# The second layer's experts computed for each token's two choices, in 15 sorted tiles, in place of all eight experts for all tokens

## The chip, the cores and the metric

The kernel runs on one core of one Trainium2 chip. A core has TensorE (matmuls, recorded as PE, its weight loads as PEld), VectorE (DVE), ScalarE (ACT), GpSimd (POOL) and SyncE (SP, which only issues DMAs). Each engine takes its own instructions in order; semaphores order the engines among each other. The metric is the device time of one execution in microseconds; less is better.

## The reference

Eight batches of 512 tokens with 128 features pass two layers. Each layer is a mixer and a mixture of experts, each behind a layer norm with a learned shift and scale, and each result is gated and added to x. Layer 0's mixer is causal attention, layer 1's a state-space scan (256 channels, 16 states). Layer 0's experts are small (64 hidden units). What the change touches is layer 1's expert block, with E = 8, F = 512, D = 128, TOP_K = 2:

```python
logits = xf @ gate_w
top_w, top_idx = jax.lax.top_k(logits, TOP_K)
top_w = jax.nn.softmax(top_w.astype(jnp.float32), axis=-1).astype(x.dtype)
combine = jnp.zeros((t, e), x.dtype).at[jnp.arange(t)[:, None], top_idx].add(top_w)
h = jax.nn.gelu(jnp.einsum('td,edf->tef', xf, w1) + b1, approximate=False)
y = jnp.einsum('tef,efd->ted', h, w2) + b2
out = jnp.einsum('ted,te->td', y, combine)
```

The reference computes every expert for every token; `combine` is zero but for two experts of each token.

## The kernel before

All tensors are fp32 but for some small bf16 operands. A batch is one iteration; the instruction streams of the five engines are written out by hand, and the order in each stream is the order of work. Batch b goes through three stages:

- attention of layer 0: 32 units (`UNITS`, numbered n), each a score matmul with a mask matmul (L701, L703), a row maximum on VectorE (L1335), an exponential on ScalarE (L1006) and transposes (L711). Between the units stand pieces of batch b - 1: the end of its mixer, its last layer norm (`norm_step`, j = 3), its choice of experts (`expert_head`, at the units in `PE_HEAD`, `ACT_HEAD`, `DVE_HEAD`), and `finish` of batch b - 2 (at unit `FINISH`), which gates the sum of the experts (L1181) and adds x (L1184).
- the middle stage: output of attention, layer norm 1, router and experts of layer 0, layer norm 2 (j = 2; rows normalised at L1214, transposed at L586), input projection, convolution, softplus. In between, projections of batch b + 1, and expert work of batch b - 1 by `early`.
- the scan of layer 1, 16 steps over two halves: decays on ScalarE (L1078), injected inputs and sums on GpSimd (L447, L466), `tensor_tensor_scan` and a product on VectorE (L1482, L1162), sums on TensorE (L663, L872). GpSimd injects three steps ahead. Between the steps TensorE does expert pieces of batch b - 1 (`SCAN_HIDDEN`, `SCAN_OUTPUT`), ScalarE gelus (`SCAN_GELU`, between two table loads) and VectorE additions (`SCAN_ADD`).

Layer 1's experts before: for each of 8 experts, 4 matmuls of 128 hidden units by 512 tokens (`hid1`, L602), a gelu with bias each (L933), and for each of 4 token tiles 4 accumulating matmuls of 128 columns (`out1`, L618). VectorE adds each expert's tile to `expert_sum`, scaled by the token's gate (`add_expert`, L1174). `w1` and `w2` (2 MB each) are loaded at the start and stay. The last batch has no later batch to stand beside: its experts follow its scan.

SP's queue carries, for each batch, the copies of the keys of batch b + 1 (`place_keys`, L379), then the rows that are broadcast for the scan (`spread_rows`, L407, 512 KB each, eight a batch). GpSimd's queue carries loads of x, stores of results, the gating of weights, and then its part of the scan (`sum_states`).

## Time and profile before

| | us |
|---|---|
| median of 3 runs | 1379.67 (1378.98 to 1379.79) |
| the profiled execution | 1379.79 |
| its span, first to last instruction | 1379.8 |
| a batch, from one scan's start to the next | 157.8 to 159.4 |
| mean granted TensorE clock | 0.950 |

A window's row gives start:end, length, each engine's busy us and records (x), granted clock, DMA share and GB/s; a sum or mean row runs over several windows. "Busy" is the time in which at least one instruction of the engine or group ran; the mean of one can be longer, because instructions overlap in the pipeline.

### The profile page before, as it was taken

The page shows a single profiled execution, that of the slowest core. Times are in us where ns is not written, and L with a number is a line of the kernel's source. Part 1 is how long each engine was busy: PE and PEld are TensorE (multiplying, and loading weights), DVE is VectorE, ACT ScalarE, POOL GpSimd, SP SyncE. Part 2 cuts the span into 40 slices and gives each one's busy share as a digit, 9 for nine tenths or more (in the row PEclk, how much of TensorE's full clock was granted, in tenths as well). Part 3 has the DMA queues.
Part 4 walks back from the last instruction along what each step waited for, and adds up shares of the span by engine and source line. Part 5 has one row for each costly group of instructions (what it writes and reads, how often), then busy time and mean ns, then how long its engine had stood idle before and what let it go on. Part 6 is the DMA issues. An engine that isn't in the chain of part 4 may idle for free. (4 is left out here: it accounts for less than half of the span.)

```text
span 1379.8 us, 19465 instructions
## 1 busy us (share of the span) xinstructions
PE 1207.2 (87%) x6560; PEld 760.5 (55%) x6560; DVE 1037.0 (75%) x2381; ACT 852.2 (62%) x1600; POOL 489.3 (35%) x309
## 2 busy tenths in 40 slices
PE   5974689989998889989999889989899899889698
PEld 3651145655665556555656456655656556555456
DVE  3666977599866997589866997579975998569822
ACT  2634446488646966489565866479664876469332
POOL 0103930078002950069100960049300870029300
PEclk8995579999999999999999999999999999999899
DMA  7101100030001200020001200021000300011000
GB/s 245 70 16 64 60 8 1 16 108 16 16 17 55 69 12 6 16 92 31 17 9 43 88 1 17 16 78 47 16 1 16 109 16 9 1 64 60 8 1 8
DMA packets 18514, 53.22 MB, mean 39 GB/s; under 512 B 4976, under 2 KB 5864, under 8 KB 18032
## 3 DMA queue, kind: packets, MB, share of 16 engines
q1 hardware_dynamic: 16112, 43.40, 9.8%
q0 software_dynamic: 1296, 4.20, 1.0%
q10 hardware_dynamic: 1008, 4.38, 0.8%
q8 instruction: 53, 0.87, 0.3%
q14 instruction: 45, 0.37, 0.1%
HBM read 45.40 MB, written 2.38 MB: 35 GB/s over the span
## 5 line engine op out<-in xcount | busy, mean ns | idle before, releaser
L1482 DVE TENSOR_TENSOR_SCAN probs_T<-bank,probs_T 128x512 f32<-128x512 f32 x256 | 303.9, 1212 | 16.1 <-ACT bank L1078 12.1
L618 PEld LDWEIGHTS bank<-w_w,hidden 128*128 128x128 f32 x2048 | 248.8, 192 | 72.9 <-issue 66.8
L602 PE MATMUL bank<-hT,w_w 128*128 128x512 f32 x512 | 262.9, 629 | 27.1 <-ACT hidden L933 26.2
L447 POOL TENSOR_TENSOR probs_T<-step_space,probs_T 128x1024 f32<-128x1024 f32 x120 | 282.2, 2358 | 5.9 <-DVE probs_T L1482 5.7
L618 PE MATMUL bank<-w_w,hidden 128*128 128x128 f32 x2048 | 251.6, 276 | 2.1 <-DVE expert_sum L1174 1.6
L933 ACT ACTIVATE hidden<-bank,w_b 128x512 f32<-128x512 f32 x256 | 169.6, 686 | 117.5 <-PE bank L602 116.9
L1006 ACT ACTIVATE probs<-bank,row_neg 128x128 f32<-128x128 f32 (+3 forms) x256 | 134.8, 528 | 151.7 <-DVE row_neg L1335 134.8
L1078 ACT ACTIVATE bank<-step_space,a_neg 128x512 f32<-128x512 f32 x256 | 167.8, 683 | 55.0 <-DVE probs_T L1482 36.7
L701 PE MATMUL bank<-k_pad,q_lat 128*128 128x512 f32 (+3 forms) x512 | 185.3, 448 | 5.8 <-DMA k_pad<-xc 5.8
L1335 DVE TENSOR_REDUCE row_neg<-bank 128x1 f32<-128x128 f32 (+3 forms) x256 | 123.5, 487 | 85.1 <-PE bank L703 82.7
L602 PEld LDWEIGHTS bank<-hT,w_w 128*128 128x128 f32 x512 | 89.0, 194 | 153.0 <-ACT hidden L933 97.0
L466 POOL TENSOR_TENSOR step_space<-step_space,probs 128x512 f32<-128x512 f32 x112 | 142.1, 1269 | 66.2 <-DVE probs L1162 66.1
L663 PE MATMUL bank<-probs,w_ident 128*128 128x512 f32 x256 | 146.0, 654 | 9.1 <-DVE probs L1162 9.1
L1162 DVE TENSOR_TENSOR probs<-probs_T,bank 128x1024 f32<-128x1024 f32 x128 | 153.2, 1197 | 0.4 <-PE bank L663 0.3
L711 PE MATMUL bank<-w_ident,probs 128*128 128x128 f32 x640 | 112.7, 278 | 8.6 <-DVE probs_T L1344 7.8
L1174 DVE SCALAR_TENSOR_TENSOR expert_sum<-bank,gates,expert_sum 128x128 f32<-128x128 f32 x256 | 71.4, 341 | 64.0 <-PE bank L618 62.5
L472 POOL TENSOR_TENSOR gated_out<-w_out_w,gate 128x256 f32<-128x256 f32 x8 | 5.8, 722 | 285.0 <-DVE xn L1214 285.0
L711 PEld LDWEIGHTS bank<-w_ident,probs 128*128 128x128 f32 x640 | 69.9, 142 | 59.1 <-issue 31.0
L872 PE MATMUL bank<-split,select 96*128 96x512 bf16 x128 | 52.7, 412 | 48.5 <-DVE probs L1162 45.7
L701 PEld LDWEIGHTS bank<-k_pad,q_lat 128*128 128x128 f32 x512 | 82.4, 200 | 14.8 <-issue 14.0
L982 ACT ACTIVATE probs_T<-bank 128x128 f32<-128x128 f32 (+3 forms) x176 | 73.8, 420 | 18.3 <-PE bank L711 17.5
L445 POOL TENSOR_TENSOR probs_T<-step_space,probs_T 128x512 f32<-128x512 f32 x16 | 23.3, 1459 | 169.3 <-DVE step_space L1471 169.3
(183 smaller groups left out, 1577.6 us busy)
## 6 DMA issues: line engine op xcount, KB each, us to landing
probs_T<-b_rows_dram SPq DMA_DIRECT2D x64, 512.0 KB, 3.7
w_w<-in_w_dram ACTq DMA_DIRECT2D x2, 2048.0 KB, 14.0
k_pad<-xc SPq DMA_DIRECT2D x64, 64.0 KB, 2.0
x_in<-in_x_dram POOLq DMA_DIRECT2D x8, 256.0 KB, 3.3
gate<-gate_rows_dram SPq DMA_DIRECT2D x1, 2048.0 KB, 7.0
out_dram<-x_out POOLq DMA_DIRECT2D x7, 256.0 KB, 2.8
step_space<-in_wmod_dram SPq DMA_DIRECT2D x1, 768.0 KB, 5.6
probs_T<-in_wqT_dram SPq DMA_DIRECT2D x1, 512.0 KB, 4.1
```

The costliest lines, as they stand in the source:

```text
L447: ins = nc.gpsimd.tensor_tensor(inject[:, n % 3, :, :], u[:], row.unsqueeze(1).to_broadcast([P, DH, T]), ALU.mult)
L466: ins = nc.gpsimd.tensor_tensor(state_sum[:, 1, :], state_sum[:, 1, :], read[:, n % 2, 1, :], ALU.add)
L602: mm(hid1_bank(n)[:], w["w1"][:, n // C1, n % C1 * P:(n % C1 + 1) * P], hT[3][:], start=True, stop=True).then_inc(hid1_mm.sem, 1)
L618: ins = mm(to[:, t * P:(t + 1) * P], hidden[:, (e * C1 + c) % (2 * C1), t * P:(t + 1) * P], w["w2"][:, e * C1 + c, :], start=(c == 0), sto ...
L663: mm(bank[SUM_BANK][:], ident[:], read[:, n % 2, 0, :], start=(n == 0), stop=(n == NS - 1)).then_inc(sum_mm.sem, 1)
L701: mm(s[:, 0:(i + 1) * P], q_lat[:, g, i * P:(i + 1) * P], k_pad[:, g, j, 0:(i + 1) * P], start=True, stop=False)
L711: ins = tr(bank[4 + n % 2][:, k * P:(k + 1) * P], probs_ring[:, n % 4, k * P:(k + 1) * P], ident[:])
L933: f(hidden[:, n % (2 * C1), :], hid1_bank(n)[:], ACT.Gelu, bias=w["b1"][:, n:n + 1]).then_inc(hid1_act.sem, 1)
L1006: f(probs_ring[:, n % 4, 0:(i + 1) * P], bank[SCORE_BANK[n % 4]][:, 0:(i + 1) * P], ACT.Exp, bias=row_neg[:, n % 4:n % 4 + 1], accum_out=r ...
L1078: f(decay(k)[:], delta[:, c, :], ACT.Exp, scale=a_neg[:, c, n:n + 1]).then_inc(dec_ok.sem, 1)
L1162: tt(read[:, n % 2, :, :], state[:, n % 2, :, :], bank[C_BANK][:].unsqueeze(1).to_broadcast([P, DH, T]), ALU.mult).then_inc(rd_ok.sem, 1)
L1482: v.tensor_tensor_scan(state[:, n % 2, c, :], decay(DH * n + c)[:], inject[:, n % 3, c, :], 0.0, ALU.mult, ALU.add).then_inc(st_ok.sem, 1)
```

## The change

A token's two choices are two pairs. The 1,024 pairs of a batch are sorted by expert into tiles of 128 rows, an expert's pairs beginning a new tile; at most 8 + 7 = 15 tiles (`NTL`) are needed, and always 15 are computed.

- `expert_head` on TensorE counts, with bf16 matmuls, the pairs that stand before each one; `place_pairs` on VectorE makes of that a row number for each pair (`slots`) and an expert for each tile (`tile_expert`).
- `scatter` on GpSimd writes the normalised rows (`xn_rows`) into a table in DRAM with eight indirect DMAs of 128 rows; SP fetches them back in groups of four tiles (`fetch_rows`), TensorE transposes them (`turn_rows`) and ScalarE applies shift and scale (`modulate_rows`).
- SP reads each tile's expert into a register and fetches that expert's two weight matrices, 512 KB, and biases (`fetch_tile`) into one of four buffers; from the fifth tile on it waits until an earlier tile's output is done.
- `hid1` and `out1` work on a tile: 4 + 4 fp32 matmuls of 128 columns, and five bf16 matmuls that add the biases, which are kept as three bf16 parts.
- ScalarE copies four tiles' results and stores them in DRAM (`save_rows`). `gather` on GpSimd, ahead of the next batch's load, fetches each pair's row with eight indirect DMAs; `add_pairs` in `finish` scales and adds the two rows of a token. `finish` moves from unit 5 to unit 14 and runs for batch b - 2 as before.
- `x_mid` gets two buffers, `w1`, `w2` and the dense gates of layer 1 go. At the start 1 MB of zeros is written to the table before the first keys are placed, and the biases are split on VectorE within batch 0's attention.

The diff, cut (declarations, signals, most waits, the removed bodies and the last batch's order are left out):

```diff
+NTL = (2 * T) // P + E - 1
+GT = 4
+TW = 4
...
+            def fetch_tile(b, i):
+                if i == 0:
+                    sp.wait_ge(tiles_ok.sem, tiles_ok.at(b, 1))
+                expert = sp.value_load(tile_expert[0:1, i:i + 1], min_val=0, max_val=E - 1)
+                if i >= TW:
+                    sp.wait_ge(out1_mm.sem, out1_mm.at(b, i - TW + 1))
+                s = tile_read[i % TW].sem
+                sp.dma_start(tile_w[:, i % TW, :], io["wcat"][bass.ds(expert, 1), :, :].rearrange("a p f -> p (a f)")
+                             ).then_inc(s, 16)
+                sp.dma_start(tile_b[0:3, i % TW, :], bias_dram[bass.ds(expert, 1), :, :].rearrange("a k f -> k (a f)")
+                             ).then_inc(s, 16)
+            def fetch_rows(b, j):
+                if j == 0:
+                    sp.wait_ge(rows_sorted.sem, rows_sorted.at(b, 16 * 2 * NT))
+                if j >= 2:
+                    sp.wait_ge(turned_mm.sem, turned_mm.at(b, j - 1))
+                n = len(tiles_of(j))
+                sp.dma_start(rows_in[:, j % 2, 0:n, :],
+                             sorted_dram[GT * j * P:(GT * j + n) * P, :].rearrange("(t p) d -> p t d", p=P)
+                             ).then_inc(rows_read[j % 2].sem, 16)
...
+                    if b > 0:
+                        for i in range(*FETCH_TILES.get(p, (0,))):
+                            fetch_tile(b - 1, i)
+                        if p in FETCH_ROWS:
+                            fetch_rows(b - 1, 2 + FETCH_ROWS.index(p))
...
+            for b in range(B):
+                if b > 0:
+                    for i in range(TW):
+                        fetch_tile(b - 1, i)
+                    for j in range(2):
+                        fetch_rows(b - 1, j)
+                if b < B - 1:
+                    place_keys(b + 1)
+                if b > 0:
+                    for i in range(TW, FETCH_FIRST):
+                        fetch_tile(b - 1, i)
                 spread_rows(b)
...
+            def scatter(b):
+                pool.wait_ge(slots_ok.sem, slots_ok.at(b, 1))
...
+                for t in range(NT):
+                    for k in range(2):
+                        nc.gpsimd.indirect_dma_start(
+                            sorted_dram[:, :], bass.IndirectOffsetOnAxis(slots[:, k, t:t + 1], 0), xn_rows[:, t, :], None,
+                            bounds_check=NTL * P - 1).then_inc(rows_sorted.sem, 16)
...
+            def gather(b):
+                for s in rows_saved:
+                    pool.wait_ge(s.sem, s.at(b, s.per_batch))
...
+                if b >= 2:
+                    gather(b - 2)
+                if b < B - 1:
+                    load(b + 1)
+                if b >= 2:
+                    store(b - 2)
+                scatter(b - 1)
...
+            def turn_rows(b, j):
+                pe.wait_ge(rows_read[j % 2].sem, rows_read[j % 2].at(b, 16 * (j // 2 + 1)))
+                if j >= 1:
+                    pe.wait_ge(hid1_act.sem, hid1_act.at(b, GT * j - 1))
+                for k in range(len(tiles_of(j))):
+                    ins = tr(turned_bank(j)[:, k * P:(k + 1) * P], rows_in[:, j % 2, k, :], ident[:])
+                ins.then_inc(turned_mm.sem, 1)
...
+            def hid1(b, i):
+                j, k = divmod(i, GT)
...
+                    to = hid1_bank(i)[:, c * P:(c + 1) * P]
+                    mm(to, tile_w[:, i % TW, c * P:(c + 1) * P], rows_T[:, j % 2, k * P:(k + 1) * P], start=True, stop=False)
+                    ins = mm(to, tile_b[0:3, i % TW, c * P:(c + 1) * P], ones_bf[0:3, :], start=False, stop=True)
...
+            def out1(b, i):
+                j, k = divmod(i, GT)
+                to = bank[ROWS_BANK[j]][:, k * P:(k + 1) * P]
...
+                    mm(to, hidden[:, i % HR, c * P:(c + 1) * P], tile_w[:, i % TW, F1 + c * P:F1 + (c + 1) * P],
+                       start=(c == 0), stop=False)
+                mm(to, ones_bf[0:3, :], tile_b[0:3, i % TW, F1:], start=False, stop=True).then_inc(out1_mm.sem, 1)
...
+                early(turn_rows, 0)
+                early(hid1, 0, 1)
...
+                early(hid1, 2)
...
+                early(out1, 0, 1, 2)
...
+                early(out1, 3)
...
+            def gelu1(b, i):
+                act.wait_ge(hid1_mm.sem, hid1_mm.at(b, i + 1))
...
+                f(hidden[:, i % HR, :], hid1_bank(i)[:], ACT.Gelu).then_inc(hid1_act.sem, 1)
...
+            def modulate_rows(b, j):
+                n = len(tiles_of(j)) * P
+                act.wait_ge(turned_mm.sem, turned_mm.at(b, j + 1))
...
+                f(rows_T[:, j % 2, 0:n], turned_bank(j)[:, 0:n], ACT.Identity, bias=mod[:, 1, 3, bass.ds(b, 1)],
+                  scale=mod[:, 1, 4, bass.ds(b, 1)]).then_inc(turned_out.sem, 1)
...
+            def save_rows(b, j):
+                of_group = tiles_of(j)
+                n = len(of_group)
...
+                f(rows_out[:, j % 2, 0:n * P], bank[ROWS_BANK[j]][:, 0:n * P], ACT.Copy).then_inc(out1_out.sem, 1)
...
+                act.dma_start(result_dram[GT * j * P:(GT * j + n) * P, :].rearrange("(t p) d -> p t d", p=P),
+                              rows_out[:, j % 2, 0:n * P].rearrange("p (t d) -> p t d", d=P)
+                              ).then_inc(rows_saved[j % 2].sem, 16)
...
+                    rest, least = (tile_w[0:E, k, 0:BIAS_W] for k in range(2))
+                    cp(tile_b[:, 0, :], w["bcat"][:]).then_inc(bias_split, 1)
+                    dve.wait_ge(bias_split, 1)
+                    tt(rest, w["bcat"][:], tile_b[:, 0, :], ALU.subtract).then_inc(bias_split, 1)
+                    dve.wait_ge(bias_split, 2)
+                    cp(tile_b[:, 1, :], rest).then_inc(bias_split, 1)
+                    dve.wait_ge(bias_split, 3)
+                    tt(least, rest, tile_b[:, 1, :], ALU.subtract).then_inc(bias_split, 1)
+                    dve.wait_ge(bias_split, 4)
+                    cp(tile_b[:, 2, :], least).then_inc(bias_split, 1)
...
+            def add_pairs(b, link):
+                dve.wait_ge(rows_fetched.sem, rows_fetched.at(b, 16 * 2 * NT))
+                for t in range(NT):
+                    link(ts(expert_sum[:, t, :], rows_back[:, 0, t, :], pair_share[:, 0, t:t + 1], None, ALU.mult))
+                for t in range(NT):
+                    link(stt(expert_sum[:, t, :], rows_back[:, 1, t, :], pair_share[:, 1, t:t + 1], expert_sum[:, t, :],
+                             ALU.mult, ALU.add))
...
+                mark, link, check = linker(dve, chain_sum, b)
+                add_pairs(b, link)
...
+            def place_pairs(b, link):
+                wide = [P, NT, E]
+                dve.wait_ge(rank_mm.sem, rank_mm.at(b, 1))
+                rank = bank[MISC][:, 0:NT * E].rearrange("p (t e) -> p t e", e=E)
+                total = bank[MISC][:, NT * E:NT * E + E]
+                link(tt(n_pairs[:], total.unsqueeze(2).to_broadcast([P, E, NT]),
+                        w["steps"][:, 0:NT].unsqueeze(1).to_broadcast([P, E, NT]), ALU.is_gt))
+                link(v.reduce_sum(n_tiles[:], n_pairs[:], AX_X))
+                link(v.tensor_tensor_scan(tile_end[:], w["steps"][:, NT + NTL:], n_tiles[:], 0.0, ALU.mult, ALU.add))
+                link(tt(first_tile[:], tile_end[:], n_tiles[:], ALU.subtract))
+                link(stt(r_b[:], first_tile[:].unsqueeze(1).to_broadcast(wide), float(P), rank, ALU.mult, ALU.add))
+                for k, pick in enumerate((pick1, pick2)):
+                    link(tt(r_a[:], pick[:], r_b[:], ALU.mult))
+                    link(v.reduce_sum(slot_at[:, k, :], r_a[:], AX_X))
+                cp(slots[:], slot_at[:]).then_inc(slots_ok.sem, 1)
+                link(tt(ended[:], w["steps"][:, NT:NT + NTL].unsqueeze(2).to_broadcast([P, NTL, E]),
+                        tile_end[:].unsqueeze(1).to_broadcast([P, NTL, E]), ALU.is_ge))
+                link(v.reduce_sum(tile_past[:], ended[:], AX_X))
+                ts(tile_expert[:], tile_past[:], float(E - 1), None, ALU.min).then_inc(tiles_ok.sem, 1)
...
+                if k == 1:
+                    finish(B - 2)
...
+LAST_SUM, LAST_READ, PE_MIXER, DVE_MIXER, FINISH, TAKE_X, NORM_UNIT = 3, 2, 6, (3, 7), 14, 8, 8
+PE_HEAD, ACT_HEAD, DVE_HEAD = (16, 18, 22), (17, 21), (20, 22, 24)
+SCAN_HIDDEN = {0: (5, 6), 2: (6, 8), 4: (8, 9), 5: (9, 10), 7: (10, 12), 9: (12, 13), 10: (13, 15)}
+SCAN_OUTPUT = {1: (4, 5), 2: (5, 6), 4: (6, 8), 6: (8, 9), 8: (9, 11), 10: (11, 12), 11: (12, 13), 13: (13, 15)}
+SCAN_TURN = (3, 8)
+SCAN_GELU = {2: (4, 6), 7: (6, 8), 12: (8, 10), 17: (10, 12), 22: (12, 14), 27: (14, 15)}
+SCAN_MODULATE = (10, 20)
+SCAN_SAVE = (13, 25, 31)
+FETCH_FIRST = 5
+FETCH_TILES = {2: (5, 7), 3: (7, 9), 4: (9, 11), 5: (11, 13), 6: (13, 15)}
+FETCH_ROWS = (1, 3)
```

## Rows read from the trace of the kernel before

**Rows 1.** The page's first part: span, busy time of each engine

```profile
span 1379.8 us, 19465 instructions
...
PE 1207.2 (87%) x6560; PEld 760.5 (55%) x6560; DVE 1037.0 (75%) x2381; ACT 852.2 (62%) x1600; POOL 489.3 (35%) x309
```

**Rows 2.** Windows, the seven scans with experts: us, busy us of each engine

```profile
sum 425.70, PE 376.43 PEld 227.11 DVE 409.94 ACT 358.06 POOL 372.74; mean PE 53.78 PEld 32.44 DVE 58.56 ACT 51.15 POOL 53.25
```

**Rows 3.** Windows, the seven middle stages of batches 1 to 7

```profile
sum 339.30, PE 321.69 PEld 203.88 DVE 211.22 ACT 184.34 POOL 31.23; mean PE 45.96 PEld 29.13 DVE 30.17 ACT 26.33 POOL 4.46
```

**Rows 4.** Windows, five attention stages of batches 2 to 6

```profile
sum 245.30, PE 222.86 PEld 151.85 DVE 195.78 ACT 149.15 POOL 14.93; mean PE 44.57 PEld 30.37 DVE 39.16 ACT 29.83 POOL 2.99
```

**Rows 5.** Windows, batch 0's middle stage and scan, the last batch's experts

```profile
78.20:128.60 50.40, 32.02 (x105) 15.94 (x103) 29.02 (x88) 18.86 (x30) 4.56 (x4) 0.74 0.12 38
...
128.60:183.30 54.70, 33.58 (x44) 9.81 (x45) 53.05 (x47) 21.56 (x31) 52.95 (x30) 0.50 0.17 53
...
1314.60:1379.80 65.20, 57.41 (x328) 39.94 (x327) 14.56 (x55) 21.18 (x32) 1.42 (x2) 0.99 0.02 5
```

**Rows 6.** Groups by line, whole span: busy us, mean ns, idle before

```profile
L602 PE MATMUL bank<-hT,w_w 128*128 128x512 f32 x512 | 262.9, 629 | 27.1 <-ACT hidden L933 26.2 <-ACT hT L939 0.9
...
L618 PE MATMUL bank<-w_w,hidden 128*128 128x128 f32 x2048 | 251.6, 276 | 2.1 <-DVE expert_sum L1174 1.6
...
L1174 DVE SCALAR_TENSOR_TENSOR expert_sum<-bank,gates,expert_sum 128x128 f32<-128x128 f32 x256 | 71.4, 341 | 64.0 <-PE bank L618 62.5 <-issue 0.7
...
L703 PEld LDWEIGHTS bank<-mask_bf,ident_bf 128*128 128x128 bf16 x256 | 25.9, 101 | 25.7 <-issue 15.3
...
L447 POOL TENSOR_TENSOR probs_T<-step_space,probs_T 128x1024 f32<-128x1024 f32 x120 | 282.2, 2358 | 5.9 <-DVE probs_T L1482 5.7
...
L1184 DVE TENSOR_TENSOR x_out<-x_mid,expert_out 128x512 f32<-128x512 f32 x7 | 4.8, 691 | 0.2
...
L472 POOL TENSOR_TENSOR gated_bias<-w_out_b,gate 128x128 f32<-128x128 f32 x8 | 3.6, 454 | 21.5 <-DVE x L1440 21.5
```

**Rows 7.** Timeline, middle stage of batch 5: start, us, instructions

```profile
889.34 3.84 PE L602 MATMUL bank<-hT,w_w 128*128 128x512 f32 x8
...
892.53 1.12 DVE L1214 TENSOR_SCALAR xn<-x,meanvar,rstd 128x128 f32<-128x128 f32 x4
...
898.30 0.60 PE L586 MATMUL bank<-w_ident,xn 128*128 128x128 f32 x4
```

**Rows 8.** Timeline, middle stage of batch 0

```profile
101.44 1.11 DVE L1214 TENSOR_SCALAR xn<-x,meanvar,rstd 128x128 f32<-128x128 f32 x4
...
102.70 1.08 PE L586 MATMUL bank<-w_ident,xn 128*128 128x128 f32 x4 [4.29 <-DVE xn L1214]
```

**Rows 9.** One line's DMA issues and the page's landing times

```profile
L523 POOL DMA_DIRECT2D out_dram<-x_out x2: 706/712/717, 1374.0 to 1375.7; - x2
...
x_in<-in_x_dram POOLq DMA_DIRECT2D x8, 256.0 KB, 3.3
...
probs_T<-b_rows_dram SPq DMA_DIRECT2D x64, 512.0 KB, 3.7
```

**Rows 10.** Timelines of GpSimd, VectorE and SP, attention and middle stage of batch 6

```profile
981.87 1.27 POOL L466 TENSOR_TENSOR step_space<-step_space,probs 128x512 f32<-128x512 f32 x1 [2.11 <-DVE probs L1162]
...
998.27 1.36 DVE L1335 TENSOR_REDUCE row_neg<-bank 128x1 f32<-128x512 f32 x2
...
1036.22 8.44 SPq L379 DMA_DIRECT2D k_pad<-xc  x8
```

**Rows 11.** Timeline, the last batch's experts

```profile
1309.56 3.78 PE L602 MATMUL bank<-hT,w_w 128*128 128x512 f32 x4 [0.87 <-ACT hT L939]
...
1314.60 0.19 DVE L1222 COPY logits<-bank 128x32 f32<-128x32 f32 x1 [7.09 <-PE bank L594]
...
1317.96 0.19 DVE L1249 TENSOR_TENSOR gates<-r_a,r_b 128x32 f32<-128x32 f32 x1
...
1373.88 0.61 DVE L1174 SCALAR_TENSOR_TENSOR expert_sum<-bank,gates,expert_sum 128x128 f32<-128x128 f32 x2 [0.21 <-PE bank L618]
```

More of the change, by code:

```diff
@@ L680, in main, with early @@
             def main(b, behind, ahead, ending):
[L682 removed]
+                def early(what, *which):
                     if behind:
[L685 to L689 removed]
+                        for i in which:
+                            what(b - 1, i)
                 def scores(n):
@@ L839, in main @@
                        ).then_inc(in_mm.sem, 1)
-                early(1, out=True, tiles=(0, 1))
+                if behind and ahead:
+                    pe.wait_ge(v_out.sem, v_out.at(b + 1, 1))
+                early(out1, 0, 1, 2)
                 for c in range(DH):
@@ L844, in main @@
                 ins.then_inc(pr_mm.sem, 1)
-                early(1, out=True, tiles=(2,))
+                early(out1, 3)
                 pe.wait_ge(pr_out.sem, pr_out.at(b, 1))
@@ L850, in main @@
                        ).then_inc(dt_mm.sem, 1)
[L851 to L853 removed]
+                early(turn_rows, 1)
+                early(hid1, 4)
             def scan(b, behind):
```

416 lines of the change are left out of this document (213 added, 203 removed).

## The prediction

> **What bounds the kernel now.** I read the page's first part, then the busy time by stage, the groups by line, the timeline of one batch and the DMA issues. The page gives TensorE 87% of the span and VectorE 75% [rows 1]. That is an average over stages that are limited by different things, so I cut the trace at the first scan and the first score of each batch; a batch then repeats three stages.
>
> The scan stage (seven with expert work beside them) lasts 425.70/7 = 60.8 us, with VectorE busy for 58.6 of them, GpSimd 53.3, TensorE 53.8 [rows 2]. VectorE sets it. Batch 0's scan, which has no experts beside it, takes 54.7 us with VectorE at 53.05, although TensorE's clock is granted at 0.50, its 1.2 GHz level [rows 5].
>
> The middle stage (from the end of attention to the scan) lasts 339.30/7 = 48.5 us with TensorE busy for 46.0 [rows 3]. It looks TensorE-bound. But batch 0 needs 50.4 us for the same stage with 32.0 us of TensorE work at a clock of 0.74 [rows 5]: a chain of layer norms, routing, convolution and softplus sets the length, and expert matmuls fill its gaps. They delay it at one place: the normalised rows of the third layer norm are finished at 893.65, the fill started at 889.34 still runs, and their transposes begin at 898.30 [rows 7]. In batch 0 the same wait is 102.70 - 102.55 = 0.15 us [rows 8].
>
> The attention stage lasts 245.30/5 = 49.1 us, TensorE 44.6, VectorE 39.2 [rows 4]. After the last scan comes the last batch's expert work alone, 65.2 us from the choice of experts, TensorE 57.4 [rows 5].
>
> **The change part by part.**
>
> TensorE work. An fp32 matmul makes two records, so one of 512 columns costs 262.9/256 = 1.03 us and one of 128 costs 251.6/1024 = 0.246 [rows 6]. Before: 32 x 1.03 + 128 x 0.246 = 64.4 us a batch. After: 120 x 0.246 = 29.5, 15 transposes at no more than 0.246 = 3.7, and 75 bf16 bias matmuls. The nearest row to those is the mask matmul's weight load, 25.9/256 = 0.101 [rows 6]: 7.6 us. Together 40.8, so 23.6 us a batch vanish, nearly 190 in all. Little of that is on a path: only the 4.5 us of waiting transposes and the last batch.
>
> Scans. Five experts' additions leave VectorE: 20 x 71.4/256 = 5.6 us [rows 6], so 58.6 becomes 53.0, batch 0's value. Floor: batch 0's 54.7. Ceiling: nothing gained, 60.8, if the new waits refill the gap. These are: tile fetches wait on SP for earlier tiles' outputs and stand ahead of the broadcast rows that GpSimd needs; a 512 KB transfer lands after 3.7 us [rows 9], and two tiles fetched between two row transfers leave about one of the three scan steps that GpSimd runs ahead. ScalarE gains three copies with a DMA issue each and loses nine gelus. TensorE keeps about 42 of 56 us. I take 1.3 us over the floor, 56.0: 7 x 4.8 = **-33.6 us**.
>
> The clock belongs here. It was 0.97 to 1.00 in scans that TensorE nearly filled and 0.50 throughout a scan in which it had 33.6 us of work at that level [rows 2, 5]. The work left would take 84 us at that level, more than the stage, so it cannot idle there as batch 0's did; I count single dips in the 1.3 us. The Trainium skill, "TensorE: Matmul & The Clock Gate", Part 1, has the low level as the default that activity lifts; the trace agrees with its 0.50 in the idle scan.
>
> Middle stages. The fill ahead of the waiting transposes becomes four row transposes (1.0), ScalarE's modulation (some 1.1) and two tiles' first matmuls (2 x 4 x 0.347 = 2.8): from 889.34 to 894.2, so they start 4.1 us earlier [rows 6, 7]. Given back: a bigger piece before the input projection (0.4), three output tiles that outlast the convolution (0.9), and a low-clock stretch early in the stage, where the removed fill had kept TensorE busy (0.3). Net 2.5, between 0 and 4: **-17.5 us** for seven.
>
> Attention. TensorE gets about 1 us lighter. VectorE loses the last expert's four additions (1.1) but gets the placing of pairs (12 linked steps at 0.22, from the 3.55 us that 16 such steps take between 1314.60 and 1318.15 [rows 11]) and eight linked additions at 0.34 [rows 6], and `finish` moves from unit 5 to unit 14 as one block of 4.4 us. Behind it on VectorE stand row maxima, for which ScalarE's exponentials and then TensorE wait. Three units of lead cover half. I take +1, between -2 and +3: **+6 us** for six.
>
> That assumes the gather has landed. GpSimd can start it after its last addition, 983.14, and unit 14 is reached at 998.3 [rows 10], a microsecond earlier without the additions. Of 14.7 us, 3.3 are a landing [rows 9]: eight indirect transfers may cost g = 1.43 us each for nothing; above that, 8 us per us of g in six batches. No row shows an indirect transfer. Below, a plain one from GpSimd, 0.712 for 256 rows of 512 bytes [rows 9]; above, GpSimd's dearest instruction, 2.36 [rows 6]. It is nearest to the plain one with a list of 128 numbers to read; the smallest read GpSimd does takes 0.454 [rows 6], so 0.71 + 0.45 plus a little, **g = 1.25**. The scatter has room: ten units after 998.3, at 49.1/32 = 1.5 us each, placing 2.4 and 10 + 3.3 for the transfers end at 1029.3; the key copies, which stand behind it on SP, begin at 1036.2 [rows 4, 9, 10]. The mixer's output matmuls newly wait for ScalarE's last copy of results; it stands behind the last decay, which ends before the last scan does, so I cost it at nothing.
>
> Start. Five linked steps split the biases on VectorE in batch 0's attention, some 4 us, half covered: **+2**. Four MB of weights leave the initial loads; one MB of zeros is written before the first key copies. I call those even, within 3.
>
> The last batch, nothing to hide behind. Four records of first matmuls (3.78) no longer precede the router [rows 11], so the choice starts at 1310.8 and takes 3.1. `finish` of the batch before now stands there: 8 x (0.341 + 0.03, what a linked step takes beyond its own 0.19 [rows 11]) + 2 x 0.69 = 4.4 [rows 6]. Weights and places 11 x 0.22 = 2.4: 1320.7. Scatter 8 x 1.25 + 3.3: 1334.0. Row fetch 3.8, transposes and modulation at the low clock 2: 1339.8. Fifteen tiles at 8 x 0.246 + 5 x 0.101 = 2.47, with transposes 3.7 and gaps 2.4: 43, to 1382.8. Copy and save 3.9, gather 10 + 3.3, additions 3: 1403.0. From the last addition to the end it was 1379.8 - 1374.5 = 5.3 [rows 1, 11]: 1408.3. **+28.5 us.**
>
> Sum: -33.6 - 17.5 + 6 + 2 + 28.5 = -14.6. The profiled execution took 1379.79, its span 1379.8, and stands 0.1 above the median of the runs: about 1365.
>
> **The rivals.**
>
> *Indirect transfers are dear* (slower). Same kernel, g larger: 16 us per us of g in the last batch and 48 beyond 1.43. The saving of 14.6 is gone at 16(g - 1.25) + 48(g - 1.43) = 14.6, g = 1.61. At 2.36: 1365 + 18 + 45 = 1428. For it: the addresses come from a list, one for each row. Against: 256 rows go out in 0.712, so a row alone costs little [rows 9]. Chance 0.22. In the extreme, each index is a separate read: the Trainium skill, "GPSIMD Engine Reference", section 7, gives about 102 cycles that do not overlap for such reads; 128 at its 1.2 GHz are 10.9 us, an estimate from that page, and the kernel would end near 1,970. No run here shows it; of the 0.22 I give it 0.02.
>
> *The scans do not shorten*: SP's fetches, ScalarE's copies or TensorE's waits for tiles put back what VectorE loses. 1365 + 33.6 = 1399. For it: four engines all above 50 of 60.8 us [rows 2] and an order on SP that couples GpSimd to TensorE. Against: batch 0's scan runs at 54.7 with a slow TensorE [rows 5]. Chance 0.14, most of it for a part of that price.
>
> *Everything hides*: scans at 54.7 (-9), middle stages at their 3.5 (-7), g = 0.71 (-8.6): 1340. For it: GpSimd idles through the attention and middle stages, 3.0 and 4.5 us busy [rows 3, 4]. Chance 0.18.
>
> **How the numbers follow.** The forecast has 0.46. Below 1338 and above 1408 I leave 0.08 and 0.12, the far ends of the third rival and of the first. Within 0.2% (2.8 us, what a measurement here can tell): 0.08, from the edges of the cases. Faster: 0.42 of the forecast, 0.18, and 0.07 of the two slower rivals where they are mild, 0.67. Slower: 0.25.
>
> **What would show it.** Scans near 56 us with VectorE at 53; the third layer norm's transposes within 0.5 us of their rows; `finish` finding the gather done; an indirect transfer near 1.25 us on GpSimd; the last batch some 27 us longer. The prediction is wrong if an indirect transfer costs over 1.61 us, if VectorE waits for broadcast rows or decays in the scans, or if TensorE runs at its low level in them.

## The result, and the profile after

The changed kernel takes 1732.89 us (median of 4 runs, 1731.57 to 1746.23) against 1379.33 before (the three runs above and a fourth): a ratio of 1.2602, interval 1.2552 to 1.2652 (the two medians alone give 1.256). The forecast was 1365, the range 1338 to 1408: wrong in direction, and by 368 us.

The page's first part of the changed kernel, beside [rows 1]:

```profile
span 1732.0 us, 20905 instructions
...
PE 1382.1 (80%) x6608; PEld 884.6 (51%) x6608; DVE 1017.9 (59%) x2276; ACT 775.7 (45%) x1507; POOL 626.1 (36%) x437
```

TensorE was to lose nearly 190 us of work; its busy time rose by 175. The busy time of VectorE and ScalarE fell by 19 and 77 us, and both idle more. The stages, as windows of the changed kernel: sums over the seven scans, the seven middle stages, the five attention stages, and the last batch from its choice of experts to the end (columns as in [rows 2 to 5]):

```profile
sum 595.60, PE 501.22 PEld 316.36 DVE 373.96 ACT 314.88 POOL 370.96; mean PE 71.60 PEld 45.19 DVE 53.42 ACT 44.98 POOL 52.99
...
sum 374.60, PE 314.04 PEld 199.93 DVE 203.58 ACT 158.59 POOL 33.63; mean PE 44.86 PEld 28.56 DVE 29.08 ACT 22.66 POOL 4.80
...
sum 291.60, PE 240.91 PEld 162.77 DVE 213.03 ACT 148.69 POOL 99.23; mean PE 48.18 PEld 32.55 DVE 42.61 ACT 29.74 POOL 19.85
...
1578.20:1732.00 153.80, 94.35 (x338) 67.03 (x338) 13.16 (x51) 15.42 (x25) 18.55 (x19) 0.50 0.23 75
```

| | before | forecast | after | difference to before, in all |
|---|---|---|---|---|
| a scan | 60.8 | 56.0 | 85.1 | +170 (seven) |
| a middle stage | 48.5 | 46.0 | 53.5 | +35 (seven) |
| an attention stage | 49.1 | 50.1 | 58.3 | +46 (five) |
| last batch, from the choice | 65.2 | 97.5 | 153.8 | +89 |
| the rest | | | | +12 |

Of the rest, 8.8 us are the sixth attention stage, batch 7's, and 5.3 the time up to batch 1's middle stage; the end of the mixer behind the last scan is 2.0 shorter.

VectorE's busy time in a scan is the 53 us of the forecast, yet the scan lasts 85. The groups by line say what it waits for, and what that waits for; first VectorE's state scan in the kernel before, then the changed kernel:

```profile
L1482 DVE TENSOR_TENSOR_SCAN probs_T<-bank,probs_T 128x512 f32<-128x512 f32 x256 | 303.9, 1212 | 16.1 <-ACT bank L1078 12.1 <-POOL probs_T L445 1.5 <-POOL probs_T L447 1.1
...
L1649 DVE TENSOR_TENSOR_SCAN probs_T<-bank,probs_T 128x512 f32<-128x512 f32 x256 | 302.7, 1212 | 216.9 <-ACT bank L1214 206.5 <-POOL probs_T L560 8.6 <-POOL probs_T L558 1.5
...
L742 PE MATMUL bank<-rows_T,tile_w 128*128 128x128 f32 x960 | 311.4, 419 | 63.9 <-issue 32.0 <-DMA tile_b<-bias_parts_dram 24.3 <-ACT rows_T L1060 7.7
...
L1052 ACT ACTIVATE hidden<-bank 128x512 f32<-128x512 f32 x120 | 71.7, 597 | 340.1 <-PE bank L743 339.5
L543 POOL DMA_INDIRECT rows_back<-result_rows_dram,slots x64 | 67.4, 1054 | 126.1 <-DMA result_rows_dram<-rows_out 107.6 <-issue 18.3
L533 POOL DMA_INDIRECT sorted_rows_dram<-xn_rows,slots x64 | 63.9, 999 | 141.7 <-DVE slots L1424 124.6 <-issue 17.1
```

VectorE's state scan stands idle for 217 us, 206.5 of them until ScalarE's decays (L1214) come; in the kernel before it was 16 and 12. ScalarE's gelus (L1052) wait 340 us for the bias matmul (L743) that ends a tile's first layer. TensorE's first-layer matmuls wait 24 us for fetched weights. The indirect transfers take 1.00 and 1.05 us each: the unknown price g, for which the slower rival stood, is not the cause.

A scan shows how this hangs together. ScalarE's timeline, batch 3's scan:

```profile
702.29 0.69 ACT L1214 ACTIVATE bank<-step_space,a_neg 128x512 f32<-128x512 f32 x1 [0.42 <-DVE probs_T L1649]
703.00 1.28 ACT L1226 ACT_TABLE_LOAD   x1
709.23 0.60 ACT L1052 ACTIVATE hidden<-bank 128x512 f32<-128x512 f32 x1 [4.95 <-PE bank L743]
712.99 0.60 ACT L1052 ACTIVATE hidden<-bank 128x512 f32<-128x512 f32 x1 [3.16 <-PE bank L743]
713.61 1.28 ACT L1229 ACT_TABLE_LOAD   x1
714.90 1.30 ACT L1214 ACTIVATE bank<-step_space,a_neg 128x512 f32<-128x512 f32 x2
```

Two gelus stand in one burst between two table loads, and the next decay stands behind them: from 702.98 to 714.90 none is made, though the gelus take 1.2 us. Three decays are made ahead; VectorE runs out of them and stands still for 7.77 us.

What TensorE does in that time is seen best in the last batch, where nothing else runs. Timeline of the changed kernel, and the window of the 15 tiles:

```profile
1641.02 0.10 PEld L743 LDWEIGHTS bank<-ones_bf,tile_b 3*128 3x128 bf16 x1 [0.22 <-issue]
1641.02 0.28 PE L743 MATMUL bank<-ones_bf,tile_b 3*128 3x128 bf16 x1
1641.23 0.50 PEld L742 LDWEIGHTS bank<-rows_T,tile_w 128*128 128x128 f32 x2
1641.23 0.80 PE L742 MATMUL bank<-rows_T,tile_w 128*128 128x128 f32 x2
...
1641.96 0.10 PEld L743 LDWEIGHTS bank<-ones_bf,tile_b 3*128 3x128 bf16 x1 [0.22 <-issue]
1641.96 0.28 PE L743 MATMUL bank<-ones_bf,tile_b 3*128 3x128 bf16 x1
...
1604.00:1703.00 99.00, 92.86 (x326) 66.03 (x326) 0.00 (x0) 13.45 (x23) 0.00 (x0) 0.50 0.21 72
```

An fp32 matmul of 128 columns with its bias matmul takes 1641.96 - 1641.02 = 0.94 us. Each weight load starts together with its matmul, not ahead of it, and TensorE's clock is granted at 0.50, its 1.2 GHz level, for the whole 99 us, in which it is busy for 93. Where the clock is up, the pair takes 852.20 - 851.63 = 0.57 us, as here in a middle stage; 0.246 + 0.101 = 0.347 was expected:

```profile
851.63 0.49 PE L742 MATMUL bank<-rows_T,tile_w 128*128 128x128 f32 x2
...
852.20 0.49 PE L742 MATMUL bank<-rows_T,tile_w 128*128 128x128 f32 x2
```

### The profile page after: what moved, and what is told of

It reads as the page before. It is cut to its first block and busy times, and to the rows that moved or that the text cites. A ratio compares the mean times of both kernels' runs of the same rounds, so it can differ in the third digit from the quotient of the medians.

```text
span 1732.0 us, 20905 instructions
## 1 busy us (share of the span) xinstructions
PE 1382.1 (80%) x6608; PEld 884.6 (51%) x6608; DVE 1017.9 (59%) x2276; ACT 775.7 (45%) x1507; POOL 626.1 (36%) x437
## 5 line engine op out<-in xcount | busy, mean ns | idle before, releaser
L1649 DVE TENSOR_TENSOR_SCAN probs_T<-bank,probs_T 128x512 f32<-128x512 f32 x256 | 302.7, 1212 | 216.9 <-ACT bank L1214 206.5
L742 PE MATMUL bank<-rows_T,tile_w 128*128 128x128 f32 x960 | 311.4, 419 | 63.9 <-issue 32.0
L742 PEld LDWEIGHTS bank<-rows_T,tile_w 128*128 128x128 f32 x960 | 203.8, 259 | 143.5 <-issue 77.3
L1052 ACT ACTIVATE hidden<-bank 128x512 f32<-128x512 f32 x120 | 71.7, 597 | 340.1 <-PE bank L743 339.5
L836 PE MATMUL bank<-k_pad,q_lat 128*128 128x512 f32 (+3 forms) x512 | 198.5, 476 | 3.9 <-DMA k_pad<-xc 3.9
L1214 ACT ACTIVATE bank<-step_space,a_neg 128x512 f32<-128x512 f32 x256 | 167.8, 683 | 47.6 <-DVE probs_T L1649 36.6
L754 PE MATMUL bank<-tile_w,hidden 128*128 128x128 f32 x960 | 172.3, 336 | 17.3 <-ACT rows_out L1072 17.3
L754 PEld LDWEIGHTS bank<-tile_w,hidden 128*128 128x128 f32 x960 | 155.6, 241 | 59.0 <-issue 43.2
L799 PE MATMUL bank<-probs,w_ident 128*128 128x512 f32 x256 | 178.0, 785 | 9.1 <-DVE probs L1321 9.1
L1003 PE MATMUL bank<-split,select 96*128 96x512 bf16 x128 | 62.7, 490 | 82.3 <-DVE probs L1321 79.6
L743 PE MATMUL bank<-ones_bf,tile_b 3*128 3x128 bf16 x480 | 124.0, 258 | 0.0
L533 POOL DMA_INDIRECT sorted_rows_dram<-xn_rows,slots x64 | 63.9, 999 | 141.7 <-DVE slots L1424 124.6
L543 POOL DMA_INDIRECT rows_back<-result_rows_dram,slots x64 | 67.4, 1054 | 126.1 <-DMA result_rows_dram<-rows_out 107.6
```

The costliest lines, as they stand in the source:

```text
L742: mm(to, tile_w[:, i % TW, c * P:(c + 1) * P], rows_T[:, j % 2, k * P:(k + 1) * P], start=True, stop=False)
L743: ins = mm(to, tile_b[0:3, i % TW, c * P:(c + 1) * P], ones_bf[0:3, :], start=False, stop=True)
L754: mm(to, hidden[:, i % HR, c * P:(c + 1) * P], tile_w[:, i % TW, F1 + c * P:F1 + (c + 1) * P], start=(c == 0), stop=False)
L799: mm(bank[SUM_BANK][:], ident[:], read[:, n % 2, 0, :], start=(n == 0), stop=(n == NS - 1)).then_inc(sum_mm.sem, 1)
L836: mm(s[:, 0:(i + 1) * P], q_lat[:, g, i * P:(i + 1) * P], k_pad[:, g, j, 0:(i + 1) * P], start=True, stop=False)
L1214: f(decay(k)[:], delta[:, c, :], ACT.Exp, scale=a_neg[:, c, n:n + 1]).then_inc(dec_ok.sem, 1)
```

## The experiments

Theory A: the bias matmuls over three rows are what is dear. Theory B: tiles wait for their weights. Theory C: TensorE has too little work left to hold the upper clock. The first four runs set them against each other; a stage's length is always its mean over windows that are cut as for the table above. Every run up to "All of it together" is a single execution, and so is "Three rows again"; the four of the changed kernel lie within 15 us of each other, so a difference below that decides nothing here.

**No bias matmuls.**

```diff
-                    mm(to, tile_w[:, i % TW, c * P:(c + 1) * P], rows_T[:, j % 2, k * P:(k + 1) * P], start=True, stop=False)
-                    ins = mm(to, tile_b[0:3, i % TW, c * P:(c + 1) * P], ones_bf[0:3, :], start=False, stop=True)
+                    ins = mm(to, tile_w[:, i % TW, c * P:(c + 1) * P], rows_T[:, j % 2, k * P:(k + 1) * P], start=True, stop=True)
...
-                mm(to, ones_bf[0:3, :], tile_b[0:3, i % TW, F1:], start=False, stop=True).then_inc(out1_mm.sem, 1)
+                ins.then_inc(out1_mm.sem, 1)
```

> This kernel leaves out the five bias matmuls of each tile, so that the experts' biases are missing from the output; fetches and order stay. Theory A (the matmuls over three rows are what is dear: a pair of an fp32 matmul and a bias matmul takes 0.57 us at the upper clock and 0.94 at the lower, where 0.344 was expected): a tile costs 8 x 0.246 = 2.0 us, VectorE sets the scans again at 57 to 60 us, the last batch shortens by some 45 us and runs at the upper clock; about 1480 us. Theory B (tiles wait for their weights): scans stay above 80 us, about 1700. Theory C (TensorE has too little work to hold the upper clock, whatever the bias matmuls look like): the last batch stays at 0.50, a tile costs 8 x 0.43 = 3.4, scans near 65; about 1540.

1502.74 us: 230 less. Scans 70.1, middle stages 44.8, attention 58.0, last batch 93.3 at a clock of 0.70, and at 1.00 in most of its tiles. Windows of the last batch and of a part of its tiles:

```profile
1407.60:1500.90 93.30, 32.62 (x263) 30.84 (x263) 13.11 (x51) 15.40 (x25) 18.49 (x19) 0.70 0.39 123
...
1444.00:1452.00 8.00, 6.97 (x62) 6.78 (x61) 0.00 (x0) 2.88 (x5) 0.00 (x0) 1.00 0.82 267
```

A is right on the last batch and on the middle stages, C is wrong; but A's scans of 57 to 60 did not come.

**Bias matmuls over all 128 rows.**

```diff
-        tile_b = sb("tile_b", [E, TW, BIAS_W], BF16)
+        tile_b = sb("tile_b", [P, TW, BIAS_W], BF16)
...
-                    ins = mm(to, tile_b[0:3, i % TW, c * P:(c + 1) * P], ones_bf[0:3, :], start=False, stop=True)
+                    ins = mm(to, tile_b[:, i % TW, c * P:(c + 1) * P], ones_bf[:], start=False, stop=True)
```

> The same number of bias matmuls, but over all 128 rows, with zeros in the 125 rows that hold no bias. Theory A (it is the three rows): a pair takes 0.34 us, as the score matmul and its mask take in attention; scans 57 to 62 us, about 1500. If the dear thing is instead the change from fp32 to bf16 and back, a pair stays at 0.57 and 0.94 and the time at 1733. Theory B (tiles wait for their weights): 1733. Theory C (too little work for the upper clock): 0.50 in the last batch, scans 75 to 85, about 1680.

1560.88 us: 172 less with the same number of matmuls, of the same columns and types. Timelines of this kernel in its last batch, first still at the lower clock and then at the upper, and the window of its 15 tiles:

```profile
1485.85 0.31 PE L744 MATMUL bank<-ones_bf,tile_b 128*128 128x128 bf16 x1
1485.85 0.55 PEld L743 LDWEIGHTS bank<-rows_T,tile_w 128*128 128x128 f32 x2
1485.95 0.74 PE L743 MATMUL bank<-rows_T,tile_w 128*128 128x128 f32 x2
1486.28 0.15 PEld L744 LDWEIGHTS bank<-ones_bf,tile_b 128*128 128x128 bf16 x1
1486.49 0.31 PE L744 MATMUL bank<-ones_bf,tile_b 128*128 128x128 bf16 x1
...
1499.93 0.22 PE L744 MATMUL bank<-ones_bf,tile_b 128*128 128x128 bf16 x1
...
1500.26 0.22 PE L744 MATMUL bank<-ones_bf,tile_b 128*128 128x128 bf16 x1
...
1482.00:1533.00 51.00, 41.20 (x330) 38.32 (x330) 0.00 (x0) 13.91 (x23) 0.00 (x0) 0.92 0.47 147
```

The pair takes 0.64 (1486.49 - 1485.85) and at the upper clock 0.33 (1500.26 - 1499.93). The bias's weights load 0.2 us ahead of their matmul, beside the one before. The clock rises to 0.92 over that window, and the tiles take 45 us (1484.65 to 1529.90) instead of 98 (1604.66 to 1702.69). It is the three rows, not the change of type: A.

**One bias matmul a tile, over 15 rows.**

```diff
+                mm(hid1_bank(i)[:], tile_b[:, i % TW, :], bias_at[:, 0:F1], start=True, stop=False, skip_group_check=True)
                 for c in range(C1):
-                    to = hid1_bank(i)[:, c * P:(c + 1) * P]
-                    mm(to, tile_w[:, i % TW, c * P:(c + 1) * P], rows_T[:, j % 2, k * P:(k + 1) * P], start=True, stop=False)
-                    ins = mm(to, tile_b[0:3, i % TW, c * P:(c + 1) * P], ones_bf[0:3, :], start=False, stop=True)
+                    ins = mm(hid1_bank(i)[:, c * P:(c + 1) * P], tile_w[:, i % TW, c * P:(c + 1) * P],
+                             rows_T[:, j % 2, k * P:(k + 1) * P], start=False, stop=True, skip_group_check=True)
```

> The four bias matmuls of a tile's first layer become one over 15 rows and 512 columns ahead of the four fp32 matmuls; the one of the second layer stays, over 15 rows. Theory A (dear is each change to a matmul over few rows): two such places a tile are left in place of five, so 2.0 + 0.2 + 2 x 0.3 = 2.8 us a tile at the upper clock; scans 58 to 63, about 1510, and less if the clock rises in the last batch. Theory B (tiles wait for their weights): above 1690. Theory C (too little work for the upper clock): last batch at 0.50, about 1570.

1566.70 us, as with 128 rows: two changes of rows a tile cost little. Scans 76.9, not 58 to 63.

**Four fetches a batch.**

```diff
                 if i >= TW:
-                    sp.wait_ge(out1_mm.sem, out1_mm.at(b, i - TW + 1))
+                    return
```

> Bias matmuls as they are, but only the first four tiles of a batch fetch weights and biases; the other eleven use what lies in their buffer, so that most of the output is wrong. Nothing is fetched between the broadcast rows of a scan and no fetch waits for a tile. Theory B (tiles wait for their weights): scans near 60 us, about 1530. Theory A (the matmuls over three rows): only the 24 us of recorded waiting for fetches go, 1700 to 1710; scans stay above 80 us and the last batch at a clock of 0.50.

1711.89 us: 21 less; scans 80.5, middle stages 56.5, 3 us longer than with all fetches, last batch 154.8 at 0.51. B alone is wrong.

So A holds for 172 to 230 us of the 354. Without any bias the kernel is still 123 us slower: scans of 70, attention stages of 58. The next four runs are about these.

**No bias matmuls and four fetches.**

> Leaves out the bias matmuls and the fetches of tiles 5 to 15, so that what is left is the sorted work alone (most of the output is wrong). Against the run without bias matmuls, 1503 us with scans of 72. If the rest of the loss in the scans is waiting for weights (37 us are recorded in that run, some 5 a scan): scans 66 to 67, about 1460. If it is ScalarE, whose bursts of gelus with two table loads wait for TensorE while the decays stand behind them: scans stay at 70 to 72, about 1490. If VectorE alone were the bound, as the prediction had it: scans 56 to 58, about 1390.

This one joins the first and the fourth diff. 1449.62 us, scans 63.6: weights are 6.5 us of a scan once the bias is out, more than expected, and 7.6 us above the forecast remain.

**Finish in the middle stage**, on the kernel with 128 rows:

```diff
-                        if n == FINISH and ending:
-                            finish(b - 2)
...
                 tt(x[:], x[:], gated_bias[:].to_broadcast([P, NT, P]), ALU.add).then_inc(bias_added.sem, 1)
+                if b >= 2:
+                    parts = linker(dve, chain_sum, b - 2)
+                    add_pairs(b - 2, parts[1])
...
+                if b >= 2:
+                    finish_x(b - 2, parts)
                 dve.wait_ge(pr_out.sem, pr_out.at(b, 1))
```

(`finish_x` is the rest of `finish`; GpSimd's store moves behind its gating of weights, and the pairs' shares get two buffers.)

> On the kernel with bias matmuls over 128 rows (1561 us, attention 57.7): finish leaves the attention stage; its eight additions go behind layer norm 2 and its last two steps behind the convolution, in the middle stage, where VectorE waits 2.8 us at each place. Theory: the block of 4.2 us on VectorE stops TensorE for 4 us, the clock falls to its lower level behind it, and the two together make the 8.4 us that an attention stage became longer: stages at 50 to 52, middle stages at most 1.5 longer, about 1520. Rival: what lengthens attention is the placing of pairs on VectorE or GpSimd's 16 indirect transfers: 56 or more, about 1555.

1502.25 us: 59 less. Attention 51.4 instead of 58.0, middle stages 45.5 instead of 45.7: the block caused 6.6 of the 8.9 us by which attention had grown, and the middle stage hides it; 2.3 remain. Another 23 us came in the scans, 73.0 instead of 76.3; why was not tried. The five attention stages with 128 rows alone, then with finish in the middle stage:

```profile
sum 290.20, PE 239.23 PEld 163.02 DVE 214.55 ACT 148.39 POOL 99.65; mean PE 47.85 PEld 32.60 DVE 42.91 ACT 29.68 POOL 19.93
...
sum 257.10, PE 223.96 PEld 150.22 DVE 194.57 ACT 147.17 POOL 95.39; mean PE 44.79 PEld 30.04 DVE 38.91 ACT 29.43 POOL 19.08
```

What the block did is seen in the changed kernel: VectorE's timeline, and the windows of TensorE's stop and of the time behind it:

```profile
596.96 1.25 DVE L1328 TENSOR_SCALAR expert_sum<-rows_back,pair_share 128x128 f32<-128x128 f32 x4
598.24 1.51 DVE L1330 SCALAR_TENSOR_TENSOR expert_sum<-rows_back,pair_share,expert_sum 128x128 f32<-128x128 f32 x4
599.79 0.69 DVE L1339 TENSOR_TENSOR rows_back<-expert_sum,gate 128x512 f32<-128x512 f32 x1
600.51 0.69 DVE L1341 TENSOR_TENSOR x_out<-x_mid,rows_back 128x512 f32<-128x512 f32 x1
...
598.60:602.90 4.30, 0.30 (x5) 0.10 (x3) 4.13 (x10) 1.06 (x3) 0.79 (x1) 1.00 0.01 3
602.90:611.20 8.30, 8.28 (x60) 5.78 (x60) 4.50 (x21) 3.79 (x14) 0.00 (x0) 0.59 0.10 30
```

No wait is marked at 596.96: the gathered rows were there. TensorE stops for 4 us, and behind the stop its clock is granted at 0.59 for 8.3 us of full work.

**Fetches ahead of the scan; gelus two decays later**, each alone on the kernel with 128 rows:

```diff
-FETCH_FIRST = 5
-FETCH_TILES = {2: (5, 7), 3: (7, 9), 4: (9, 11), 5: (11, 13), 6: (13, 15)}
+FETCH_FIRST = 7
+FETCH_TILES = {2: (7, 8), 3: (8, 9), 4: (9, 11), 5: (11, 13), 6: (13, 15)}
```

```diff
-SCAN_GELU = {2: (4, 6), 7: (6, 8), 12: (8, 10), 17: (10, 12), 22: (12, 14), 27: (14, 15)}
+SCAN_GELU = {4: (4, 6), 9: (6, 8), 14: (8, 10), 19: (10, 12), 24: (12, 14), 29: (14, 15)}
```

> On the kernel with bias matmuls over 128 rows (1561 us, scans of 76 to 79): tiles 6 and 7 are fetched ahead of the scan's broadcast rows and not between them. If waiting for weights is on the scans' path: about 5 us from each, 1525. If ScalarE's bursts set the pace: within 10 us of 1561.

> On the kernel with bias matmuls over 128 rows (1561 us): each of ScalarE's six bursts of gelus in a scan stands two decays later, so that TensorE has a step more for the tiles that the burst needs. If the bursts wait for TensorE with the decays behind them (2.8 us a burst in the run without bias matmuls): scans 70 to 73, about 1515. If waiting for weights sets it: no change, 1555 to 1565. A burst that comes too late for the next tiles would make it slower, 1570 to 1590.

1501.33 and 1441.11 us: 60 and 120 less; scans 67.1 and 58.7. Both beat what was expected. VectorE's state scan with 128 rows alone, with the earlier fetches and with the later gelus, then TensorE's first-layer matmuls in the last two:

```profile
L1654 DVE TENSOR_TENSOR_SCAN probs_T<-bank,probs_T 128x512 f32<-128x512 f32 x256 | 302.6, 1212 | 152.1 <-ACT bank L1215 141.7 <-POOL probs_T L561 8.6 <-POOL probs_T L559 1.5
...
L1654 DVE TENSOR_TENSOR_SCAN probs_T<-bank,probs_T 128x512 f32<-128x512 f32 x256 | 302.5, 1212 | 111.4 <-ACT bank L1215 88.5 <-POOL probs_T L559 14.3 <-POOL probs_T L561 8.6
...
L1654 DVE TENSOR_TENSOR_SCAN probs_T<-bank,probs_T 128x512 f32<-128x512 f32 x256 | 300.3, 1210 | 24.6 <-ACT bank L1215 14.2 <-POOL probs_T L561 8.6 <-POOL probs_T L559 1.5
...
L743 PE MATMUL bank<-rows_T,tile_w 128*128 128x128 f32 x960 | 193.4, 330 | 39.7 <-issue 31.1 <-ACT rows_T L1061 7.7 <-DMA tile_b<-bias_parts_dram 0.9
...
L743 PE MATMUL bank<-rows_T,tile_w 128*128 128x128 f32 x960 | 188.6, 322 | 85.4 <-DMA tile_b<-bias_parts_dram 36.1 <-issue 31.2 <-ACT hidden L1053 9.3
```

VectorE's wait for decays falls from 141.7 us to 88.5 with the earlier fetches and to 14.2 with the later gelus. TensorE's wait for weights falls to 0.9 with the earlier fetches; with the later gelus it is 36.1, no less than the 31.4 with 128 rows alone, and yet hardly any of it reaches VectorE. So a late weight was dear where a burst of gelus, with the decays behind it, stood waiting for that tile: late weights and late matmuls are two causes of one wait.

**All of it together**, and then with one bias matmul of 128 rows and 512 columns a tile:

```diff
             for k in range(3):
-                if k == 1:
-                    finish(B - 2)
                 expert_head(B - 1, k, head)
+            finish(B - 2)
```

> Everything that the runs so far pointed to, in one kernel: bias matmuls over 128 rows, gelus two decays later, tiles 6 and 7 fetched ahead of the scan, finish in the middle stage, and the finish of the last but one batch behind the placing of pairs, where VectorE waits for rows anyway. If the causes are separate: scans 60, attention 51, middle stages 43, last batch 4 us shorter than in the run with later gelus; 1441 - 8 x 6 - 4 - 5 = about 1385, within 15 of the kernel before. If they overlap (the later gelus already gave what the earlier fetches give): 1390 to 1400. If finish in the middle stage now delays the scan: above 1400.

> The same, but with one bias matmul of 512 columns over 128 rows per tile for the first layer in place of four of 128. Columns are the same; 3 weight loads and 3 instructions fewer a tile. By the rows of the run with four of them (0.34 us a pair): 15 x 3 x 0.05 = 2 us less of TensorE a batch, on a path only in the last: 0 to 15 us less than the other kernel of this pair.

1383.82 us, ratio 1.0052 (1.0024 to 1.0080), and 1379.87 us, 1.0009 (0.9986 to 1.0032); the two intervals overlap. Windows of the first of them, scans, middle and attention stages, last batch:

```profile
sum 394.60, PE 309.85 PEld 226.12 DVE 371.21 ACT 312.18 POOL 368.67; mean PE 44.26 PEld 32.30 DVE 53.03 ACT 44.60 POOL 52.67
...
sum 327.50, PE 265.74 PEld 189.45 DVE 224.64 ACT 161.33 POOL 37.55; mean PE 37.96 PEld 27.06 DVE 32.09 ACT 23.05 POOL 5.36
...
sum 253.60, PE 220.45 PEld 148.81 DVE 193.70 ACT 147.43 POOL 94.19; mean PE 44.09 PEld 29.76 DVE 38.74 ACT 29.49 POOL 18.84
...
1290.50:1387.90 97.40, 41.51 (x338) 38.56 (x338) 13.19 (x51) 15.40 (x25) 18.49 (x19) 0.73 0.38 118
```

Scans 394.6/7 = 56.4, middle stages 46.8, attention 50.7, last batch 97.4: near the forecast's 56.0, 46.0, 50.1 and 97.5. Part of that is luck: finish no longer stands in attention, and the last batch takes 23.1 us to its first tile, 45.2 for the tiles and 29.2 behind them, where 29.0, 43 and 25.5 were forecast. Nor is the whole the forecast's: this run's span, 1387.9 us, is 8 longer than before and not 15 shorter. Up to batch 1's middle stage it takes 9.7 us more than before, where 2 were forecast (1.0 more in the run with one bias matmul a tile; what makes the difference was not tried), middle stages gain 5.7 less and six attention stages cost 5.2 more than forecast.

**Three rows again** in that kernel (`tile_b` and its matmuls as in the changed kernel):

> The kernel with all four mendings (1384 us), with the bias matmuls over three rows again. If three rows cost TensorE's time and its clock wherever the pieces stand: 172 us more as between the first two kernels, 1555, with scans near 75 and the last batch at a clock of 0.50. If the three rows hurt only because the gelus stood too early: scans near 62, and the last batch's some 40 us alone, 1460.

1526.93 us, 143 more. Scans 62.7, middle stages 54.8, last batch 148.5 at 0.51. Neither number was met: the scans are those of the second case, the last batch that of the first. Three rows cost 6.3 us a scan here and 8.8 where the gelus stood early (85.1 against 76.3), and as much as there elsewhere. The last batch:

```profile
1376.70:1525.20 148.50, 92.70 (x338) 65.96 (x338) 13.16 (x51) 15.40 (x25) 18.52 (x19) 0.51 0.24 78
```

**All experts for the last batch:**

```diff
-            for i in range(NTL):
-                if i % GT == 0:
-                    turn_rows(B - 1, i // GT)
-                hid1(B - 1, i)
-                if i >= 1:
-                    out1(B - 1, i - 1)
-            out1(B - 1, NTL - 1)
+            for n in range(2, C1 + 2):
+                all_hidden(n)
+            for e in range(E):
+                for t in range(NT):
+                    all_out(e, t)
+                for n in range((e + 1) * C1 + 2, min((e + 2) * C1 + 2, E * C1)):
+                    all_hidden(n)
```

(`all_hidden` and `all_out` are the old `hid1` and `out1` on fetched weights; the gates and the scaled additions of before return for this batch.)

> The kernel with one bias matmul of 128 rows (1380 us, 93 us from the last batch's choice of experts to the end), with the last batch's experts computed as before the change, all eight for all tokens, their weights fetched in eight transfers, the first four before the choice. No sort, no transfers of rows, TensorE at work from the choice on: the 65 us of the kernel before [rows 5] and up to 4 for the finish of the batch before. 1380 - 25 = 1355, faster than the kernel before by 1.5%. If fetching an expert's weights lags behind its matmuls (8.2 us an expert against some 6 for a transfer), up to 1370.

1365.94 us, ratio 0.9910 (0.9878 to 0.9942): 0.9% less than the kernel before, and the interval leaves 1 out. From the choice to the end it takes 71.8 us instead of 93.4, a little above the forecast's 69, with TensorE busy for 59.8 at a clock of 0.95. The whole is 14 us less, not 25, since 22 are gained here and the median lies some us above the profiled run (1363.38).

## Why the prediction was wrong, and where it was right

- **The step that failed first: the price of a bias matmul.** It was taken from the mask's weight load, 0.101 us [rows 6], though that one is over 128 rows and the bias over three. A pair of fp32 matmul and bias took 0.57 us at the upper clock and 0.94 at the lower instead of 0.347. Of this term no second bound was worked out, and no rival stood on it. The Trainium skill, "TensorE: Matmul & The Clock Gate", section "Step-by-step: what each phase is for", has weights loading while the matmul before still runs, where the groups of rows do not conflict or the load goes to a background weight buffer, in a time that does not hang on the number of rows. On the time of the load the trace agrees at the upper clock (0.09 us for 3 rows, at 851.47 of the changed kernel, and 0.10 for 128, at 1500.15 of the kernel with 128 rows), at the lower it does not (0.10 for 3, 0.15 for 128); that the load runs ahead it shows beside matmuls over 128 rows alone. Between matmuls over 128 and over three rows it did not; which of the page's conditions fails there no run here shows.
- **A possible sign of it stood in the trace of the kernel before.** There L657 adds the second layer's biases with matmuls over eight rows. Their first weight load starts with its matmul, 0.76 us behind the load before it, and the load behind them starts with its own matmul too, while other loads there run 0.1 us ahead (1318.54 for a matmul at 1318.65). TensorE waits there for ScalarE's copy of the gates as well, which was done by 1319.44, so this is a sign and no proof:

```profile
1320.46 0.96 PEld L657 LDWEIGHTS bank<-w_b,gates_T 8*128 8x128 f32 x8 [0.76 <-issue]
1320.46 1.15 PE L657 MATMUL bank<-w_b,gates_T 8*128 8x128 f32 x8
...
1321.55 0.30 PEld L602 LDWEIGHTS bank<-hT,w_w 128*128 128x128 f32 x2
1321.55 1.98 PE L602 MATMUL bank<-hT,w_w 128*128 128x512 f32 x4
```

- **"It cannot idle there as batch 0's did."** The clock was argued from work at the forecast's prices. With three rows the last batch stayed at 0.50 through 93 us of busy time; with 128 rows the same matmuls ran at 0.92 and more. That the forecast counted single dips only was wrong for scans (0.71 to 0.76), too. Why the clock stays down with three rows is not settled: the last batch ran at 0.50 or 0.51 in all three runs with them, but the pairs at 851.63, three rows as well, ran at the upper level.
- **The second step that failed: the floor of a scan and what stands in its way.** Batch 0's 54.7 us was a right floor for VectorE's work and a wrong one for the order: that scan has no gelus on ScalarE. Scans came to 85.1 instead of 56.0, and to 70.1 without any bias matmul. "The new waits" were named (fetches on SP, ScalarE's copies), but not the old one: on ScalarE decays stand behind bursts of gelus that wait for TensorE. Shifting the gelus by two decays was worth 120 us on the kernel with 128 rows, and with it a scan takes 58.7, with fetches ahead and finish moved 56.4. The rival that scans do not shorten had this mechanism half right (TensorE's waits for tiles) and its price, 1399, as a ceiling that it is not: a wait can be longer than what it takes the place of.
- **Attention, +1.** The block's 4.4 us were right (4.2), its cover of half was not. TensorE stopped for 4 us and then ran 8.3 us at 0.59; the stage became 9.2 us longer. Moved to the middle stage the block cost nothing there, and attention stages of 51.4 remained, 2.3 above before.
- **The middle stage.** In the changed kernel the third layer norm's transposes still came 857.31 - 853.83 = 3.5 us late, behind first-layer matmuls at 0.94 a pair. Without bias matmuls they came at 608.05, 0.15 us behind the rows, and the stage took 44.8, 3.7 us less than before, where 2.5 was forecast.
- **g.** An indirect transfer took 1.0 to 1.05 us and the next began 0.30 later: 1.32 instead of 1.25, below the 1.43 that is free. (By the prediction's own figures it is 1.36: 998.3 less a microsecond less 983.14 leaves 14.2 us, not 14.7. The gather stays below that too.) The gather's last was issued at 591.95, and finish at 596.96 found it landed. The Trainium skill's rule of some 102 cycles for each read ("GPSIMD Engine Reference", section 7), which stood as the extreme rival, does not bear on these: 128 indices in 1.02 us.
- **The last batch.** Choice to first tile 26.5 us and from the last tile to the end 29.3, against 29.0 and 25.5 forecast. The 15 tiles took 98.0 instead of 43; with 128 rows 45.3.
- **The prediction's own signs.** Two of its three signs of being wrong came: VectorE waits for decays in the scans (206.5 us in all), and TensorE falls to its low level in them (a clock of 0.71 to 0.76). An indirect transfer over 1.61 us did not.

So one price of work was wrong, that of a matmul whose shape goes with waiting weights and a low clock, and the rest is not work but order: instructions in places that were tuned for other lengths. From 1733, in the order in which they were tried: 172 for the rows, 59 for finish, 118 for gelus, fetches and the last finish together give 1384. The parts overlap: put back into the mended kernel, the three rows cost 143.
